# First loads ahead of the zeroed row, one-hots in pairs, positions in PSUM, and new orders on all queues

## The reference

```python
x = x + quantised_experts(layernorm(x), w1, w2)   # per batch: w1 512x512, w2 512x256
x = x + routed_ffn(layernorm(x), router_w, gate_proj, up_proj, down_proj)
```

```python
s = sqrt(max(amax_x, EPS) / max(amax_w, EPS)); xs = x / s; ws = w * s
x_q = round(xs / x_scale); w_q = round(ws / w_scale)
out = x_q @ w_q.T * x_scale * w_scale.T
```

## Time and profile before

| | us |
|---|---|
| median of 3 runs | 412.88 |
| the runs | 410.58, 438.5, 412.88 |
| the profiled execution, its own time | 408.86 |
| its span, first to last instruction | 406.9 |

### The profile page before, as it was taken

How to read it: one execution, slowest core, us unless ns; L and a number is a source line. 1 busy time by engine, 2 the same in 40 slices (tenths; PEclk the granted TensorE clock), 3 DMA queues, 4 the chain that set the end, 5 groups by cost and what they waited for, 6 DMA issues and landing times.

```text
span 406.9 us, 6243 instructions
## 1 busy us (share of the span) xinstructions
PE 343.2 (84%) x1860; PEld 204.4 (50%) x1860; DVE 233.6 (57%) x512; ACT 206.3 (51%) x386; POOL 244.3 (60%) x264
## 2 busy tenths in 40 slices
PE   5767867876987886889989988999999999999960
PEld 3435425564656753467545634555555555545420
DVE  1675888799698999875855674333333333333310
ACT  1439669968776657151942545344444343434330
POOL 5374896999577965266237314546667666666340
PEclk9898989998699599895999999999999999999995
DMA  6840934739546562203471373655876567766552
GB/s 207 278 163 16 345 156 146 268 102 363 155 157 217 197 207 67 89 26 87 103 226 27 53 234 105 120 107 88 151 123 118 98 111 131 116 138 108 82 70 26
DMA packets 26590, 56.77 MB, mean 140 GB/s; under 512 B 2560, under 2 KB 12800, under 8 KB 24512
## 3 DMA queue, kind: packets, MB, share of 16 engines
q0 software_dynamic: 8736, 20.45, 27.9%
q1 hardware_dynamic: 17824, 35.93, 25.3%
HBM read 37.50 MB, written 18.87 MB: 139 GB/s over the span
## 4 chain that ended last, share of the span: by engine, by line
PE 48%; DVE 24%; POOL 8%; issue 7%; ACT 6%; DMA 4%; POOLq 0%; DVEq 0%; SPq 0%; ACTq 0%
PE bank_h L1255 19%; PE bank_q L1276 9%; DVE rmax L725 5%; PE bank_q L1127 4%; PE bank_t L1240 3%; DVE amax L695 3%; PE bank_t L1127 3%; PE bank_q L1178 2%; DVE xn L737 2%; DVE onehot L842 2%; PE bank_r L1212 2%; PE bank_h L1155 2%; DMA w_in<-tokens,gather_at 2%; PE bank_r L1266 1%; DVE packed L849 1%
## 5 line engine op out<-in xcount | busy, mean ns | idle before, releaser
L1255 PE MATMUL bank_h<-gu_hi,xT 128*128 x312 | 104.6, 381 | 1.4 <-DVE xT L928 1.2
L1255 PE MATMUL bank_h<-gu_lo,xT 128*128 x156 | 59.6, 382 | 0.0
L928 DVE SCALAR_TENSOR_TENSOR xT<-bank_t,xT 128x512 f16<-128x512 f32 x39 | 26.8, 690 | 53.9 <-ACT xT L1056 53.7
L1276 PE MATMUL bank_q<-dn_hi,aT 128*128 x156 | 52.8, 379 | 2.3 <-DVE aT L946 2.0
L1255 PEld LDWEIGHTS bank_h<-gu_hi,xT 128*128 128x128 f16 x312 | 30.7, 98 | 31.4 <-issue 3.0
L639 POOL DMA_INDIRECT w_in<-tokens,gather_at x30 | 29.9, 997 | 20.4 <-DVE gather_at L913 10.3
L567 POOL TENSOR_TENSOR gu_lo<-stage,gu_hi 128x1024 bf16<-128x1024 f32 x16 | 34.6, 2172 | 12.2 <-ACT gu_hi L1013 12.1
L936 DVE SCALAR_TENSOR_TENSOR gated<-bank_h,gated 128x256 f32<-128x256 f32 x39 | 16.5, 423 | 33.1 <-ACT gated L1063 33.1
L695 DVE TENSOR_REDUCE amax<-bank_t 128x1 f32<-128x512 f32 x48 | 31.0, 684 | 6.7 <-PE bank_t L1127 6.6
L660 POOL DMA_INDIRECT out<-h,scatter_at x17 | 26.9, 1584 | 13.0 <-DMA out<-h,scatter_at 4.7
L1063 ACT ACTIVATE gated<-bank_h 128x256 f32<-128x256 f32 x39 | 15.0, 384 | 37.3 <-PE bank_h L1255 37.3
(11 more groups left out here) (192 smaller groups left out, 741.0 us busy)
## 6 DMA issues: line engine op xcount, KB each, us to landing
x_in<-in_x SPq DMA_DIRECT2D x4, 1024.0 KB, 5.2
w_in<-in_fside_BxS2xS SPq DMA_DIRECT2D x4, 1024.0 KB, 5.3
stage<-in_L_ffn_gate_proj SPq DMA_DIRECT2D x8, 512.0 KB, 5.1
stage<-in_L_ffn_up_proj SPq DMA_DIRECT2D x8, 512.0 KB, 4.1
stage<-in_L_ffn_down_proj SPq DMA_DIRECT2D x8, 512.0 KB, 4.6
x<-in_x SPq DMA_DIRECT2D x4, 1024.0 KB, 6.7
out<-x SPq DMA_DIRECT2D x4, 1024.0 KB, 7.5
tokens<-xn SPq DMA_DIRECT2D x4, 1024.0 KB, 6.3
```

The lines of the kernel that those rows point to most:

```text
L928: dve.scalar_tensor_tensor(out=xT[i % 2][:, 1].rearrange("p c t -> p (c t)"), in0=bank, scalar=X_SCALE, in1=xT[i % 2][:, 0].rearrange("p c ...
L1255: ins = pe.matmul(bank, xT[i % 2][:, part, c], rhs[:, cols], start=(c == 0 and m == 0), stop=(c == C - 1 and m == 2))
L1276: ins = pe.matmul(bank, aT[i % 2][:, part, c], rhs[:, cols], start=(c == 0 and n == 0), stop=(c == FC - 1 and n == 2))
```

## The change

Six things change.

1. **First loads.** router_w is loaded from ACT's queue. On SP, x of batch 0 comes first, in four pieces with a semaphore each, then w1 in two halves; the zeroed row is stored behind `load w2 0`.
2. **Positions.** The base of each expert is added by a matmul with a matrix of 1/128 ahead of the mask's matmuls, so DVE has no addition of its own. Positions and their rounding stay in the PSUM bank of the ranks instead of SBUF.
3. **Gap.** The difference of the two best scores moves from `place` on DVE to a new stage `gap g` on POOL.
4. **Pairs.** `onehot` and `packed` are laid out with two of the four j beside each other; `packed` is made in two halves.
5. **Orders** of all five queues.
6. **Fillers**: other counts.

```diff
 FILLERS = {
-    ("w1 columns", 0): 14, ("rows 1", 0): 6, ("w1 scale row", 0): 14, ("rows 2 inverse", 0): 16,
-    ("a transposed", 1): 6, ("place", 0): 13, ("sort step", 0): 3, ("sort step", 1): 8, ("sort step", 2): 16,
-    ("sort step", 3): 4,
+    ("w1 columns", 0): 14, ("x columns", 0): 4, ("rows 1", 0): 5, ("w1 scale row", 0): 18, ("rows 1", 1): 3,
+    ("rows 2 inverse", 0): 18, ("rows 1", 2): 3, ("product 2", 0): 8, ("sort step", 0): 5, ("sort step", 1): 3,
+    ("sort step", 2): 3, ("sort step", 3): 3,
 }
```

The first loads:

```diff
-            sp.dma_start(rw[:], router_w.rearrange("(c p) e -> p c e", p=P)).then_inc(sem("router_in"), 16)
+                else:
+                    for j in range(J):
+                        sp.dma_start(x_in[:, j], x_dram[b][:, j]).then_inc(sem(f"x_piece{j}"), 16)
...
+                    for n in range(2):
+                        half = slice(n * D // 2, (n + 1) * D // 2)
+                        sp.dma_start(w1_in[:, :, half], w1_dram[b][:, :, half]).then_inc(sem(f"w1_half{n}"), 16)
```

`gap` on POOL:

```diff
+            def gap_of(g):
+                m = len(GROUPS[g])
+                first = GROUPS[g][0] % 2
+                pool.wait_ge(sem("mask_ready"), g + 1)
+                pool.tensor_tensor(gap[:, 0:m], best[:, 0, 0:m], best[:, 1, 0:m], ALU.subtract).then_inc(sem("gap_made"), 1)
+                pool.wait_ge(sem("gap_made"), g + 1)
+                pool.wait_ge(sem("shift1"), GROUPS[g][-1] + 1)
+                pool.tensor_tensor(gap[:, 0:m], gap[:, 0:m], rstd[:, first:first + m, 1], ALU.mult).then_inc(sem("gap_ready"), 1)
```

`place` on DVE (the `gap` operations leave; the end of the bank's use moves behind place_of):

```diff
-                then(dve.tensor_tensor(slot[:, 0:m].rearrange("p m (j e) -> p (m j) e", e=E),
-                                       rank[:, 0:m * J * E].rearrange("p (t e) -> p t e", e=E),
-                                       spread(base[g][:], [P, m * J, E], 1), ALU.add))
-                dve.tensor_tensor(base[g + 1][:], rank[:, m * J * E:(m * J + 1) * E], base[g][:], ALU.add).then_inc(ring_x.taken, 1)
+                dve.tensor_copy(base[g + 1][:], rank[:, m * J * E:(m * J + 1) * E]).then_inc(sem("base_ready"), 1)
...
+                spare = rank[:, 2 * P:2 * P + 2 * m * K * J].rearrange("p (s m k j) -> p s m k j", s=2, m=m, k=K)
+                pos, rounding = spare[:, 0], spare[:, 1]
...
-                            then(dve.tensor_tensor(onehot[:, k, s], number[:], spread(place_of[:, s, n, k], [P, P, J], 1), ALU.is_equal))
+                            then(dve.tensor_tensor(onehot[:, k, s], spread(number[:, :, 0:2], [P, J // 2, P, 2], 1),
+                                                   spread(place_of[:, s, n, k].rearrange("p (h i) -> p h i", i=2), [P, J // 2, P, 2], 2),
+                                                   ALU.is_equal))
...
-                        dve.tensor_tensor(packed[:], spread(onehot[:, k, 0], [P, 3, P, J], 1), spread(values[:, :, b, k], [P, 3, P, J], 2),
-                                          ALU.mult).then_inc(sem("packed"), 1)
+                        for half in range(2):
+                            ins = dve.tensor_tensor(packed[:, :, half], spread(onehot[:, k, 0, half], [P, 3, P, 2], 1),
+                                                    spread(values[:, :, b, k, 2 * half:2 * half + 2], [P, 3, P, 2], 2), ALU.mult)
```

PE, in `place` and in `table`:

```diff
+                    pe.wait_ge(sem("base_ready"), g)
+                pe.matmul(rank, share[:], spread(base[g][:], [P, m + 1, E], 1), start=True, stop=False)
                 pe.wait_ge(sem("mask_ready"), g + 1)
...
-                        ins = pe.matmul(bank[:, 0:3 * P].rearrange("p (v l) -> p v l", v=3), onehot[:, n % K, 1, :, j], packed[:, :, :, j],
+                        ins = pe.matmul(bank[:, 0:3 * P].rearrange("p (v l) -> p v l", v=3), onehot[:, n % K, 1, j // 2, :, j % 2],
+                                        packed[:, :, j // 2, :, j % 2],
```

More of the change, by code:

```diff
@@ L361, in block_kernel @@
             SP_ORDER[:], POOL_ORDER[:], DVE_ORDER[:], ACT_ORDER[:], PE_ORDER[:])
+        sp_order.insert(sp_order.index(("load w2", 0)) + 1, ("store pad", 0))
         first_late = pool_order.index(("gather", EARLY))
@@ L488, in store_tokens, with store_pad @@
                 sp.dma_start(tokens_out[b], xn2[:]).then_inc(sem(f"tokens_stored{b}"), 16)
-            sp.wait_ge(sem("zeroed"), 1)
-            sp.dma_start(tokens_dram[N:N + P], blank).then_inc(sem("pad_stored"), 16)
-            in_turn(sp_order, {"load x": load_x, "load w1": load_w1, "load w2": load_w2, "load x again": load_x_again,
+            def store_pad(_):
+                sp.wait_ge(sem("zeroed"), 1)
+                sp.dma_start(tokens_dram[N:N + P], blank).then_inc(sem("pad_stored"), 16)
+            in_turn(sp_order, {"store pad": store_pad, "load x": load_x, "load w1": load_w1, "load w2": load_w2, "load x again": load_x_again,
                                "store x1": store_x1, "store tokens": store_tokens, "load expert": load_expert})
@@ L664, in _ @@
                                  "root 1": partial(root, 0), "root 2": partial(root, 1), "smooth w1": smooth_w1,
-                                 "smooth w2": smooth_w2, "gate times up": gate_times_up, "residual": residual, "low": low})
+                                 "smooth w2": smooth_w2, "gate times up": gate_times_up, "residual": residual, "gap": gap_of, "low": low})
             pool.wait_ge(sem("landed"), MOST + 1)
@@ L673, in _, with moments @@
             dve.tensor_tensor(rwc[:], rw[:], spread(bank_h[:, 1, 0:E], [P, C, E], 1), ALU.subtract).then_inc(sem("centred"), 1)
-            def moments(which, src, ready, per_batch, b):
+            def moments(which, src, b):
                 st, m = stats[:, b % 2, which], mv[:, b % 2, which]
                 for j in range(J):
-                    if j < per_batch:
-                        dve.wait_ge(ready, upto(b, per_batch, j) * (16 if per_batch == 1 else 1))
+                    if which == 0 and b == 0:
+                        dve.wait_ge(sem(f"x_piece{j}"), 16)
+                    elif which == 0 and j == 0:
+                        dve.wait_ge(sem("x_in"), 16 * b)
+                    elif which == 1:
+                        dve.wait_ge(sem("x1_ready"), upto(b, J, j))
                     dve.bn_stats(st[:, j], src[:, j]).then_inc(sem(f"stats{which}"), 1)
@@ L814, in place @@
                 m, chunk = members(g)
-                dve.wait_ge(sem("shift1"), GROUPS[g][-1] + 1)
-                then(dve.tensor_tensor(gap[:, 0:m], best[:, 0, 0:m], best[:, 1, 0:m], ALU.subtract))
-                first = GROUPS[g][0] % 2
-                dve.tensor_tensor(gap[:, 0:m], gap[:, 0:m], rstd[:, first:first + m, 1], ALU.mult).then_inc(sem("gap_ready"), 1)
                 rank = ring_x.empty(dve, "place", 0, g)
@@ L848, in place @@
                             after_sort(step - 1)
-                        dve.tensor_tensor(packed[:], spread(onehot[:, k, 0], [P, 3, P, J], 1), spread(values[:, :, b, k], [P, 3, P, J], 2),
-                                          ALU.mult).then_inc(sem("packed"), 1)
+                        for half in range(2):
+                            ins = dve.tensor_tensor(packed[:, :, half], spread(onehot[:, k, 0, half], [P, 3, P, 2], 1),
+                                                    spread(values[:, :, b, k, 2 * half:2 * half + 2], [P, 3, P, 2], 2), ALU.mult)
+                            if half == 0:
+                                then(ins)
+                            else:
+                                ins.then_inc(sem("packed"), 1)
             def add_to_table(g):
@@ L1117, in keep_busy, with w1_columns @@
                     pe.matmul(bank, below[:], number[:].rearrange("p l j -> p (l j)"), start=True, stop=True)
+            def w1_columns(b):
+                for c in range(C):
+                    bank = ring_t.fill(pe, "w1 columns", c, b)
+                    if c == 0:
+                        keep_busy(bank, "w1 columns", b)
+                    if b == 0:
+                        pe.wait_ge(sem(f"w1_half{2 * c // C}"), 16)
+                    elif c == 0:
+                        pe.wait_ge(sem("w1_in"), 16 * b)
+                    for j in range(J):
+                        ins = pe.transpose(bank[:, j * P:(j + 1) * P], w1_in[:, j, c * P:(c + 1) * P], identf[:])
+                    ins.then_inc(ring_t.filled, 1)
             def transposed(ring, stage, src, n, ready, count, b):
```

56 lines of the change are left out of this document (30 added, 26 removed), and 94 rows, old and new, of tables (ACT_ORDER, DVE_ORDER, PE_ORDER, POOL_ORDER).

## The result

The changed kernel takes 398.76 us (median of 4, 396.78 to 399.72), the kernel before 411.73 (median of 4, 409.2 to 438.5). The ratio is 0.968, with a 95% interval of 0.963 to 0.973; run again in another session it was 0.966 (0.963 to 0.969). Ratios leave out the executions that ran slow as a whole, such as the one of 438.5 and the profiled ones of e2 and e11. The prediction was 395.5, in a range of 386 to 408. The direction and the mechanism held; of the 15.4 us in the sum, 9.7 came in the first profiled execution (span 397.2 for 406.9) and 13.3 in the second (393.6).

What follows compares the result with a forecast made beforehand. VectorE's queue was taken to bound choose 0 to indices 0, TensorE the tiles, an engine-changing chain the start; -0.7 - 3.5 - 8.4 - 1.7 - 1.4 - 2.7 + 3.0 = -15.4 gave 393.5 us, 395.5 as a median, range 386 to 408.

Steps and rivals of the forecast that it cites:

- Rival (a): VectorE and GpSimd still meet: 6 of 10.0 us of stalls remain, time 401.5 us; chance 0.13.
- Rival (b): Pairs give TensorE nothing, or VectorE loses two elements a cycle: 399 to 400.5 us; chance 0.10.
- Rival (c): A ScalarE and store chain ahead of gather 0 replaces VectorE's queue as bound: 404.6 to 410 us; chance 0.16.
- Rival (d): With fewer fillers TensorE's clock drops and the kernel is slower, over 421.1 us; chance 0.06.
- Start: First loads: x arrives earlier, so VectorE's statistics wait less; 0.7 us gained.
- choose 0: Two VectorE operations stalled by GpSimd fall from 1.83 and 2.08 us to about 0.2 each; 3.5 us gained.
- place 0: VectorE's stage loses its gap operations and one-hot stalls, with shorter rank products; 8.4 us gained.
- list 0 to indices 0: VectorE's stretch behind place 0: w2 columns 3 moves behind indices 0; 1.7 us gained.
- To the first tile: From indices 0's end to the first expert matmul: 13.3 us for 14.68; 1.4 us gained.
- Early tiles: Pairs shorten TensorE's sort matmuls in four steps, its other work and idle time unchanged; 2.7 us gained.
- Late tiles: Same length, as each gather has as many scatters ahead as before; 0 us, bounds -2 and +5.2.
- the 3.0 put aside: Losses: 1.5 us for gate times up 3 under place 0's one-hots, 1.5 for new idle time in the reordered middle.

Runs made afterwards that it cites:

- e2: Kernel before with only the changed routing arithmetic (one-hots in pairs, positions in PSUM, base added by matmul); ratio to before 0.992.
- e11: Kernel of e6 with 7 more fillers, none ahead of product 2 1; ratio to before 0.958.
- e1: Changed kernel with the routing arithmetic and first loads of before, keeping new orders, gap on GpSimd and new fillers; ratio to before 0.986.
- e9: Changed kernel with low 22 waiting for batch 0's first packed product, so lows 22 and 23 run under place 0; ratio to before 0.976.
- e4: Changed kernel with the old layout of one-hots and packed values (stride of 8 bytes, one packed product); ratio to before 0.978.
- e3: Kernel before with only the first loads of the changed one; ratio to before 0.996.
- e10: Changed kernel with low 20 moved behind smooth w2 2 and deviation 2 1, so it runs under choose 0; ratio to before 0.968.
- e5: Kernel before with GpSimd held by two waits so no low runs under choose 0 or place 0's one-hots; ratio to before 1.009.
- e6: Changed kernel with high 21 ahead of w1 transposed 3, x high 9 ahead of take y 7, and x low 9 ahead of a low 8; ratio 0.963.
- e8: Changed kernel with 15 more fillers where TensorE was idle ahead of a clock fall, 5 of them ahead of product 2 1; ratio to before 0.971.
- e7: Changed kernel without the 14 fillers between the sort matmuls of batch 0; ratio to before 0.975.

## Why the prediction was right, and where its sizes were off

**The direction and the mechanism were right.** Meetings made VectorE's stretch long, and the orders removed most of them (e1, e9). How much of the time this brought is less sure: 1.4% with e1. Rival (a), that they still meet, held for one pair of one-hots and one operation of `list 0`, under 2 us. Rival (b) fell: sorts at 0.85 (e4) and one-hots at 0.44 each. Rival (c): no store ended `gather 0`'s wait. Rival (d) fell: 0.96 was granted in the early tiles. In the late tiles TensorE waited for no gather. New idle time of VectorE did come, at 141 to 144, just behind the 70 to 140 that I named as the sign.

**Start, 0.7 forecast: about 1.7** (e3, up to `choose 0`; the total doesn't resolve it). The w1 columns, which I saw as cover, began as late as before (11.75 us for 11.73), but the gain of the statistics went by them: the x columns began at 15.45 for 16.52.

**choose 0, 3.5 forecast: the stalls went, the time did not.** This step failed, and it is the one to learn from. I took "busy 33.9 of 36.6" for "every us removed from this queue arrives". VectorE then waited 3.3 us for a row from ScalarE, and from the start of `choose 0` to that of `place 0` it took 11.9 us for 12.5: at most 0.6 of the 3.5 arrived. I had put 1.5 us aside for new idle time, unplaced; e10 and e5 (`place 0` 0.57 us earlier for 3.5) show that the stall and this hole are the same time. The row stands behind `w1 transposed 3` and `high 21`; with `high 21` out of the way (e6, e11) the product behind the same transposes is about as late. What makes them late stays open. TensorE's half clock (10.7 us for three stages of 16 matmuls, two of which take 1.85 and about 2.1 at full clock) is the likeliest, and e8, where the first of the three ran at full clock, has a hole of 2.0 for 3.3. But the clock fell somewhere from 130 to 145 in every run, so none shows the row without it.

**place 0, 8.4 forecast: 6.2 and 7.1 in two executions.** The length was to be 10 us. Of the rest, 1.0 is low 23, and with TensorE at half clock there were waits of 0.82 and 0.50 in the first execution (0.22 each in the second, at full clock). With low 21 moved (e6) it is 10.1.

**list 0 to indices 0.** With `w2 columns 3` gone 4.3 us should be left of before's 6.0; it took 5.6. Of the 1.3, 0.7 is an operation of `list 0` on which `gate times up 3` fell (0.97 us for 0.30) and 0.4 a new wait for TensorE ahead of `indices 0`. I named the stage and mislaid its time by 10 us, because I followed its input (`silu 3`) and not its output buffer, which TensorE had still to read for `a transposed 2`.

**To the first tile, 1.4 forecast: 0.** 14.85 and 14.33 for 14.68. `scores 5` ran at half clock again (3.49 us for 1.85, 0.50 granted in 175 to 180), which is the 1.6 us that the first execution is over my 13.3.

**Early tiles, 2.7 forecast: 0, though the pairs did all that was asked.** Without pairs the new order makes the stage 68.2 and 67.7 us (e1, e4), where the old one had 64.7. TensorE is busy 61.5 there for 59.2, at a clock of 0.95 for 0.98, and waits 1.44 and 1.64 around tile 8 for 0.55 and 0.97 before. I had written that nothing else of its work changes and kept its idle time; the pairs paid for that. In the one profile of the old order with pairs (e2) the stage isn't shorter either.

**Late tiles, 0 forecast: 0** (152.2 and 152.7 for 152.7).

The sum 15.4 and the first execution's 9.7 differ by 5.7: the early tiles and the way there 4.6, the stretch to `indices 0` 4.5, less the 3.0 put aside and 0.5 of the late tiles. Of these 5.7, 3.6 are within what two executions differ by: the second gave 13.3. That the total came so near owes something to luck: of `choose 0` and the early tiles, 6.2 us of the sum, at most 0.6 arrived, and the 3.0 put aside without a place covered about half of what was missing. The times that I named beside the sum (`indices 0` by 161, the first expert matmul near 174) leave these 3.0 out; with them the two come 1.5 and 3.1 us later than forecast.

## What to carry to other kernels

A stall taken out of a full queue arrives only as far as the next input of that queue is early: look up when the next stage's inputs end, and count the stall up to there. A blocking operation must run somewhere, so move it to a time when the blocked engine works from PSUM or waits, and follow both its input and the buffer that it writes. Fillers pay where the work behind them is on the path (e7) and cost where they stand ahead of a product that the next engine waits for (e8).

## What the runs showed of the hardware that I had not expected

An operation with a single SBUF input is stopped too: a copy of 128x8 took 2.06 us and a scalar operation 1.99 under lows 20 and 21 (e5). A reduction of float32 was not: two took 2.34 us with low 17 under them (e5, 142.50), no more than twice the 1.22 of one alone, and so did two under low 19 in the kernel before (145.32). Nor was an eviction, with one of its three inputs in PSUM: two in 1.41 us under low 21 (144.26).

Four matmuls over 16-bit operands took 1.54 us at a stride of 8 bytes (e4) and 0.85 at one of 4 (the changed kernel), both in `place 2` at a granted clock of 1.00. Both operands were strided, so which of them costs the time isn't shown.
